# Cross-attention with adapter on one Trainium2 core: four of sixteen residual adds moved from VectorE to TensorE and ScalarE

## The chip, the cores and the metric

The kernel runs on one core of one Trainium2 chip. The metric is device microseconds of one execution; the median of three runs of the kernel before is 247.23 us (247.22 to 247.85). TensorE is called PE in the rows (PEld its weight loads), VectorE DVE, ScalarE ACT, GpSimd POOL, SyncE SP.

## What is computed

Two inputs x and ctx, 32 batches of 256 tokens by 256 features. The first layer is a cross-attention whose result for batch 0 alone (`att[0]`) is added to every batch. The second layer, cut to what matters here:

```python
norm_X, norm_F = layernorm(ctx), layernorm(x)          # F is the queries
attended = softmax(norm_F @ norm_X.T / 16) @ norm_X
h = gelu(attended @ fc1.T + fc1_b)                     # 4 values per token
cross = h @ fc2.T + fc2_b
n = layernorm(cross)
self_attended = softmax(n @ n.T / 16) @ n
return norm_F + gamma2 * (cross + gamma1 * self_attended)
```

The last line's sum with `norm_F`, the queries, is the place of the change.

## The kernel before, in words

Batches are worked on in sixteen pairs, and features lie on the partitions in the end: `Fall` holds the normalized queries of all 32 batches in SBUF, 128 partitions by 2 chunks of 256 tokens per batch, fp32. A first part (to about 175 us) normalizes, does the first attention, and saves per token four hidden values.

The second part, from about 175 us, handles the self-attention. Since `cross` has rank five, its products are small: operands cut into bf16 pieces, 36 to 60 rows high. Each engine runs its own loop over steps p = 0 to 20, and within a step everything is in the order of the code. The order on TensorE in step p: `maxima_turn(p)` (L1074), `scores(p+1)` (L1063), `turn(p+2)` (L1048), `shift(p)` (L1082), `keep_busy` (L873, small fp32 products into bank 5 that nobody reads), then in even steps `attend` (L1095) and `output_turn` (L1114), in odd steps `back` (L1104), and last `output(p-5)` (L1130). `output(n)` is four bf16 products per pair, with both members in two PSUM banks, 6 and 7 for nearly all n, so the next pair has to wait until the banks are read. Pair 13 goes to banks 2 and 3, pair 15 to banks 0 and 1.

VectorE in step p: `maxima(p+1)` (L564, a reduction over 1024 columns that needs `scores(p+1)`), then `collected` (L571, even) or `returned` (L576, L579, L581, odd), then `finish(p-5)` (L586): it adds the pair's 1024 PSUM columns to `Fall`, in place, 128x1024 fp32. After that in early steps some algebra for the second half of the batches, which `turn(8)` in step 6 waits for.

ACT in step p: `maxima_turned(p)` (L830), `turned(p+2)` (L800, the copy sT), `weights(p)` (L838, the exponential of 1024 columns), and in even steps `output_turned` (L845, the copy cT). ACT's copy of L786 belongs to the first part. POOL cuts the coefficients for `output_turn` in `output_cuts` (L700 to L707), after `returned` on VectorE. SP stores each batch of `Fall` (L293) in order, once `finish` of its pair is done.

An order written by hand is all there is: no planner. Waits are semaphores; TensorE's `maxima_turn` also waits for VectorE's copy OB (L576) in even steps, `output(n)` for `finish(n-1)`, `finish(n)` for `output(n)`.

Steps of the trace that the argument uses: TensorE's turn of the maxima for step 9 starts at 209.74, that for step 10 at 212.41, that for step 11 at 215.87.

Of the kernel before, what the change touches and what calls it, by code (L numbers as in the profile page):

```python
# [24 lines left out]
ALU = mybir.AluOpType  # L25
ACT = mybir.ActivationFunctionType
# [4 lines left out]
N = 256  # L31
D = 256
NT = N // P
DC = D // P
# [12 lines left out]
GROUP = TILES // 2  # L47
LATE = {20: (0,), 22: (1,), 23: (2,), 24: (3,), 25: (4,), 26: (5,), 27: (6,), 28: (7,), 29: (8,)}
NEXT = {0: (0,), 2: (1, 2), 3: (3, 4), 4: (5, 6), 5: (7, 8)}
ASIDE = ()  # L50
SBANK1 = (0, 1, 5)
SLOTS_L = ((0, 1, 3), (3, 1, 2), (5, 1, 1))
SLOTS_R = ((0, 3, 2), (1, 3, 2), (2, 1, 1))
# [18 lines left out]
def build(nc, x, ctx, x0t, c0t, wqt, wkt, wvt, params, out):  # L72
# [5 lines left out]
    def sem(name):  # L78
        return stack.enter_context(nc.semaphore(name))
# [111 lines left out]
    exp2_ok, o2_mm, o2_saved = sem("exp2_ok"), sem("o2_mm"), sem("o2_saved")  # L191
    o2T_ok, back_mm = sem("o2T_ok"), sem("back_mm")
    ct_mm, cT_ok, f_mm, fin_ok = sem("ct_mm"), sem("cT_ok"), sem("f_mm"), sem("fin_ok")
    aside_ok, added_ok = sem("aside_ok"), sem("added_ok")
    h_ok, co_ok, sC_ok, pads_ok = sem("h_ok"), sem("co_ok"), sem("sC_ok"), sem("pads_ok")
    out_done = sem("out_done")

# [41 lines left out]
        return bank[2 * (1 - p % 2) + m]  # L239

    def own_adds(n):
        return sum(i not in ASIDE for i in range(n))

    STORED = tuple(range(PAIRS))

    def result(n):
        return {13: (2, 3), 15: (0, 1)}.get(n, (6, 7))

    def results(n):
        a, _ = result(n)  # L250
        return psum[:, 512 * a:512 * (a + 2)]

    def aside(n):
        return XT[:, (n // 2) % 2, :, :].rearrange("p c n -> p (c n)")

    def pair(n):
        return Fall[:, 2 * n:2 * n + 2, :, :].rearrange("p b c n -> p (b c n)")
# [16 lines left out]
    @block.sync  # L274
    def _(sp):
        sp.dma_start(par[:, :], params).then_inc(par_in, 16)
        for dst, src, arrived in ((x0T, x0t, q_in), (wqT, wqt, q_in), (c0T, c0t, k_in), (wkT, wkt, k_in),
                                  (wvT, wvt, v_in)):
            sp.dma_start(dst[:, :, :], src).then_inc(arrived, 16)

        for p in range(PAIRS):
            if p >= SLOTS // 2:
                sp.wait_ge(t_mm, turns_to(p - SLOTS // 2, 1))
            for src, dst, arrived in ((c_d, cN, c_in), (x_d, xN, x_in)):
                for b in (2 * p, 2 * p + 1):
                    sp.dma_start(dst[:, b % SLOTS, :], src[b, :, :]).then_inc(arrived[b % SLOTS], 16)

        for n, b in ((n, b) for n in STORED for b in (2 * n, 2 * n + 1)):
            if n in ASIDE:
                sp.wait_ge(added_ok, ASIDE.index(n) + 1)  # L290
            else:
                sp.wait_ge(fin_ok, own_adds(n) + 1)
            sp.dma_start(out_d[b, :, :], Fall[:, b, :, :].rearrange("p c n -> p (c n)")).then_inc(out_done, 16)  # L293
        sp.wait_ge(out_done, 16 * B)

    @block.vector
    def _(dve):
# [292 lines left out]
        for p in range(2 * QUADS + 5):  # L590
            if p + 1 < PAIRS:
                maxima(p + 1)
            if p % 2 == 0 and 2 <= p < 2 * QUADS + 2:
                collected((p - 2) // 2)
            if p % 2 == 1 and 3 <= p < 2 * QUADS + 3:
                returned((p - 3) // 2)
            if p >= 5 and p - 5 not in ASIDE:
                finish(p - 5)
            for part in NEXT.get(p, ()):
                algebra(1, part)  # L600

    @block.gpsimd
    def _(pool):
# [102 lines left out]
            pool.wait_ge(sC_ok, 5 * q + 4)  # L706
            pool.tensor_tensor(to[:, :, 2 * CO:3 * CO], left, to[:, :, CO:2 * CO], ALU.subtract).then_inc(sC_ok, 1)  # L707

        def add_aside(n):
            pool.wait_ge(aside_ok, ASIDE.index(n) + 1)  # L710
            pool.tensor_tensor(pair(n), aside(n), pair(n), ALU.add).then_inc(added_ok, 1)

        right(0)
        for p in range(2 * QUADS + 5):
            if p == 4:
                right(1)
            if p % 2 == 1 and 3 <= p < 2 * QUADS + 3:
                output_cuts((p - 3) // 2)
            if p - 5 in ASIDE:
                add_aside(p - 5)  # L720

    @block.scalar
    def _(act):
# [102 lines left out]
        def maxima_turned(p):  # L826
            act.wait_ge(m_mm, p + 1)
            if p >= 2:
                act.wait_ge(s2m_mm, p - 1)
            act.activation(nm2T[:, p % 2, :], bank[5][0:2 * VW, 0:P // 2].bitcast(BF16), ACT.Copy).then_inc(m_ok, 1)  # L830
# [13 lines left out]
                act.wait_ge(f_mm, 2 * q - 2)  # L844
            act.activation(cT[:, q % 2, :], bank[4][:, 0:NT * P].bitcast(BF16), ACT.Copy).then_inc(cT_ok, 1)  # L845

        def set_aside(n):
            act.wait_ge(f_mm, n + 1)
            if ASIDE.index(n) >= 2:
                act.wait_ge(added_ok, ASIDE.index(n) - 1)  # L850
            act.activation(aside(n), results(n), ACT.Copy).then_inc(aside_ok, 1)

        for p in range(2 * QUADS + 4):
            if p < PAIRS:
                maxima_turned(p)
            if p == 0:
                applied(QUADS - 1)
            if p + 2 < PAIRS:
                turned(p + 2)
            if p < PAIRS:  # L860
                weights(p)
            if p - 5 in ASIDE:
                set_aside(p - 5)
            if p == 1:
                hidden(1)
            if p % 2 == 0 and p >= 4:
                output_turned((p - 4) // 2)

    @block.tensor
    def _(pe):  # L870
        def keep_busy(n, b):
            for _ in range(n):
                pe.matmul(bank[b][:, 0:P], ident[:, :], ident[:, :], start=True, stop=True)  # L873
# [241 lines left out]
            last.then_inc(ct_mm, 1)  # L1115

        def output(n):
            pe.wait_ge(cT_ok, n // 2 + 1)
            if n == 14:
                pe.wait_ge(fin_ok, own_adds(13))  # L1120
            elif n in (13, 15):
                pe.wait_ge(exp2_ok, PAIRS)
            elif n - 1 in ASIDE:
                pe.wait_ge(aside_ok, ASIDE.index(n - 1) + 1)
            elif n >= 1:
                pe.wait_ge(fin_ok, own_adds(n))
            for c in range(DC):
                for m in range(2):
                    rows = slice(SLOT * m, SLOT * m + SC)
                    last = pe.matmul(bank[result(n)[m]][:, c * N:(c + 1) * N], RT[rows, c * P:(c + 1) * P],  # L1130
                                     cT[rows, (n // 2) % 2, (n % 2) * N:(n % 2 + 1) * N], start=True, stop=True)
            last.then_inc(f_mm, 1)

        for b in range(B + 1):
# [31 lines left out]
        for p in range(2 * QUADS + 5):  # L1166
            if p < PAIRS:
                maxima_turn(p)
            if p == 0:
                keep_busy(3, 6)  # L1170
                apply(QUADS - 1)
            if p + 1 < PAIRS:
                scores(p + 1)
            if p == 0:
                apply_back(QUADS - 1)
            if p + 2 < PAIRS:
                turn(p + 2)
            if p < PAIRS:
                shift(p)
                keep_busy(5 if p < 5 else 2, 5)  # L1180
            if p % 2 == 0:
                if 2 <= p < 2 * QUADS + 2:
                    attend((p - 2) // 2)
                if 4 <= p < 2 * QUADS + 4:
                    output_turn((p - 4) // 2)
            elif 3 <= p < 2 * QUADS + 3:
                back((p - 3) // 2)
            if p >= 5:
                output(p - 5)
# [49 lines left out]
```

## Time and profile before

| | before |
|---|---|
| median of 3 runs | 247.23 us |
| profiled execution, its own time | 246.86 us |
| its span, first to last instruction | 245.1 us |
| mean granted TensorE clock | 0.957 |
| busy: PE, PEld | 214.2 us (87%), 154.2 us (63%) |
| busy: DVE, ACT, POOL | 198.0 us (81%), 148.9 us (61%), 124.4 us (51%) |
| L586, the adds, 16 | 19.4 us, mean 1221 ns |
| L564, reductions, 16 | 19.5 us, mean 1218 ns |

The busy shares are means over both parts. The page's slices, 40 of 6.1 us each, show tenths of busy time; the second part is slices 29 to 40:

```
PE   6989989677999999999999899999978569999750
DVE  6888858899999978789899999733558958998764
PEclk9999999999999999999999999999999759999955
```

The engines' rows have one digit per slice; PEclk is the granted clock in tenths. A timeline's row gives the start, the duration, the instructions merged into it, and in brackets the engine's idle time before it and what ended that. The ends of matmuls are modelled, so on TensorE the distance between starts is the safer number.

### The profile page before, as it was taken

What the parts mean: (1) busy time and instruction counts of PE and PEld (TensorE: products, weight loads), DVE (VectorE), ACT (ScalarE), POOL (GpSimd) and SP (SyncE); (2) the same over time, 40 slices, a digit from 0 to 9 for tenths busy, and PEclk for the clock granted to TensorE, in tenths of its full rate; (3) what the DMA queues carried; (4) which work ended last, traced back from release to release, by engine and by line L of the source; (5) the groups of instructions that cost most, each with busy time, mean ns of one, the idle gap of its engine ahead of it and who ended that gap; (6) DMA issues with size and microseconds to landing.
All of it is one profiled execution on the core that took longest, in us unless ns stands there. A gap on an engine that the chain in (4) does not pass through costs nothing.

```text
span 245.1 us, 4980 instructions
## 1 busy us (share of the span) xinstructions
PE 214.2 (87%) x1758; PEld 154.2 (63%) x1758; DVE 198.0 (81%) x391; ACT 148.9 (61%) x284; POOL 124.4 (51%) x184
## 2 busy tenths in 40 slices
PE   6989989677999999999999899999978569999750
PEld 6766548446878779697787787867645225554320
DVE  6888858899999978789899999733558958998764
ACT  2167856226778678596787968846775326666310
POOL 6000096776999999969698939200002522222220
PEclk9999999999999999999999999999999759999955
DMA  6990000242455514455243000000000022444566
GB/s 186 366 350 3 1 4 0 93 143 109 173 171 148 161 56 155 174 168 174 82 151 113 3 1 3 0 1 3 0 3 1 0 88 86 173 175 174 190 238 257
DMA packets 14712, 26.81 MB, mean 109 GB/s; under 512 B 1760, under 2 KB 1760, under 8 KB 14688
## 3 DMA queue, kind: packets, MB, share of 16 engines
q1 hardware_dynamic: 14688, 26.50, 31.2%
q8 instruction: 14, 0.23, 0.4%
q14 instruction: 10, 0.08, 0.1%
HBM read 18.11 MB, written 8.39 MB: 108 GB/s over the span
## 4 chain that ended last, share of the span: by engine, by line
PE 55%; DVE 28%; issue 8%; ACT 4%; POOL 2%; DVEq 0%; POOLq 0%; ACTq 0%
PE psum L981 15%; PE psum L918 7%; DVE bn L381 6%; DVE xN L401 6%; PE psum L989 5%; PE psum L873 5%; DVE nm L564 3%; PE psum L1019 3%; PE psum L1095 3%; PE psum L931 2%; DVE nmax L524 2%; PE psum L1001 2%; PE psum L946 2%; PE psum L959 2%; PE psum L888 2%
## 5 line engine op out<-in xcount | busy, mean ns | idle before, releaser
L981 PE MATMUL psum<-XT,Fall 128*128 128x256 f32 x256 | 60.9, 381 | 1.8 <-ACT Fall L763 1.8
L981 PEld LDWEIGHTS psum<-XT,Fall 128*128 128x128 f32 x256 | 46.1, 190 | 7.2 <-ACT Fall L763 2.2
L656 POOL TENSOR_SCALAR cN<-cN,nmean,rstd 128x256 f32<-128x256 f32 x64 | 38.5, 614 | 2.4 <-POOL rstd L643 2.3
L636 POOL TENSOR_TENSOR xN<-xN,tgt 128x512 f32<-128x512 f32 x28 | 35.7, 1278 | 1.6 <-DVE xN L401 1.6
L401 DVE TENSOR_SCALAR xN<-xN,bn,rstd 128x256 f32<-128x256 f32 x64 | 33.8, 571 | 0.7 <-POOL rstd L643 0.7
L786 ACT ACTIVATE PT<-psum 128x512 f32<-128x512 f32 x32 | 19.2, 599 | 24.3 <-PE psum L989 24.2
L700 POOL CAST sC<-co 128x160 bf16<-128x160 f32 x8 | 2.6, 322 | 61.6 <-DVE co L581 61.6
L793 ACT ACTIVATE E<-psum,nmax 128x256 f32<-128x256 f32 x64 | 26.8, 475 | 10.9 <-DVE nmax L524 10.9
L524 DVE TENSOR_REDUCE nmax<-psum 128x2 f32<-128x512 f32 x32 | 22.0, 686 | 13.7 <-PE psum L981 13.2
L643 POOL TENSOR_TENSOR rstd<-vps,minus_half 128x8 f32<-128x8 f32 (+1 forms) x16 | 25.0, 1564 | 15.4 <-DVE vps L392 15.3
L760 ACT ACTIVATE XT<-psum,b1s,w1s 128x512 f32<-128x512 f32 x32 | 23.1, 794 | 3.8 <-PE psum L918 3.8
L763 ACT ACTIVATE Fall<-psum,par 128x512 f32<-128x512 f32 x32 | 23.4, 797 | 3.2 <-PE psum L918 3.2
L873 PE MATMUL psum<-ident 128*128 128x128 f32 x144 | 23.3, 308 | 1.9 <-POOL ident L608 1.9
L873 PEld LDWEIGHTS psum<-ident 128*128 128x128 f32 x144 | 19.4, 208 | 5.5 <-issue 3.6
L586 DVE TENSOR_TENSOR Fall<-psum,Fall 128x1024 f32<-128x1024 f32 x16 | 19.4, 1221 | 4.2 <-PE psum L1130 4.2
L381 DVE BATCH_NORM_STATS2 bn<-cN 128x6 f32<-128x512 f32 x32 | 22.3, 695 | 0.4 <-DVE r L457 0.2
L381 DVE BATCH_NORM_STATS2 bn<-xN 128x6 f32<-128x512 f32 x32 | 21.9, 689 | 0.0
L564 DVE TENSOR_REDUCE nm<-psum 128x4 bf16<-128x1024 f32 x16 | 19.5, 1218 | 1.5 <-PE psum L1063 1.4
L989 PE MATMUL psum<-ident,E 128*128 128x128 f32 x128 | 20.2, 280 | 0.3 <-ACT E L793 0.2
L989 PEld LDWEIGHTS psum<-ident,E 128*128 128x128 f32 x128 | 14.3, 141 | 8.3 <-issue 6.3
L918 PE MATMUL psum<-ident,xN 128*128 128x128 f32 x128 | 17.1, 274 | 2.6 <-DVE xN L401 2.3
L918 PE MATMUL psum<-ident,cN 128*128 128x128 f32 x128 | 16.9, 274 | 0.1
(157 smaller groups left out, 348.5 us busy)
## 6 DMA issues: line engine op xcount, KB each, us to landing
cN<-ctx SPq DMA_DIRECT2D x32, 256.0 KB, 2.9
xN<-x SPq DMA_DIRECT2D x32, 256.0 KB, 4.2
out<-Fall SPq DMA_DIRECT2D x32, 256.0 KB, 2.3
x0T<-x0t SPq DMA_DIRECT2D x1, 256.0 KB, 2.6
wqT<-wqt SPq DMA_DIRECT2D x1, 256.0 KB, 2.9
c0T<-c0t SPq DMA_DIRECT2D x1, 256.0 KB, 3.7
wkT<-wkt SPq DMA_DIRECT2D x1, 256.0 KB, 4.8
wvT<-wvt SPq DMA_DIRECT2D x1, 256.0 KB, 5.0
```

The source lines that it names most:

```text
L381: dve.bn_stats(bn[:, (b // 2) % 4, side, b % 2, :], src[:, b % SLOTS, :].rearrange("p (t d) -> p d t", t=NT)).then_inc(st_ok, 1)
L401: dve.tensor_scalar(own, own, stat(p, 1, m, t, 1), root_of(p, 1, m, t), ALU.subtract, ALU.mult)\
L524: dve.tensor_reduce(nmax[:, b % 2, :], tiles(bank[SBANK1[b % 3]]), AX.X, ALU.max, negate=True)\
L564: dve.tensor_reduce(nm2[:, p % 2, :, 0:NT], scored(p).rearrange("p (m t k) -> p m t k", m=2, t=NT), AX.X, ALU.max, negate=True).then_inc(m ...
L636: pool.tensor_tensor(xN[:, b % SLOTS, :], xN[:, b % SLOTS, :], tgt2[:, :, :].rearrange("p t d -> p (t d)"), ALU.add).then_inc(y_ok, 1)
L643: pool.tensor_tensor(rstd[:, p % 4, sides, :].rearrange("p s k -> p (s k)"), vps[:, p % 4, sides, :].rearrange("p s k -> p (s k)"), minus_ ...
L656: pool.tensor_scalar(own, own, nmean[:, p % 4, NT * m + t:NT * m + t + 1], root_of(p, 0, m, t), ALU.add, ALU.mult)\
L793: act.activation(E[:, b % 2, t * N:(t + 1) * N], bank[SBANK1[b % 3]][:, t * N:(t + 1) * N], ACT.Exp, bias=nmax[:, b % 2, t:t + 1]).then_in ...
L873: pe.matmul(bank[b][:, 0:P], ident[:, :], ident[:, :], start=True, stop=True)
L918: last = pe.transpose(bank[TBANK[n % 3]][:, m * N + t * P:m * N + (t + 1) * P], z[:, (2 * p + m) % SLOTS, t * D + c * P:t * D + (c + 1) * ...
L981: last = pe.matmul(bank[SBANK1[b % 3]][:, t * N:(t + 1) * N], Fall[:, b, c, t * P:(t + 1) * P], XT[:, p % 4, c, m * N:(m + 1) * N], start= ...
L989: last = pe.transpose(bank[SBANK1[b % 3]][:, k * N + t * P:k * N + (t + 1) * P], E[:, b % 2, t * N + k * P:t * N + (k + 1) * P], ident[:, :])
```

## The change

For the pairs 1, 4, 7 and 10 the sum with the queries is made in PSUM: TensorE multiplies the four 128x256 pieces of `Fall` of the pair by the fp32 identity, before the output products accumulate onto them. ACT copies the two banks back into `Fall`, one member each, one step later: the first ahead of the copy sT, the second behind the exponential. VectorE does no add for these pairs, the next pair's `output` waits for the second copy, and SP stores each member after its own copy. In the steps of these four outputs `keep_busy` is left out. The wait for cT stands behind the identity products. An unused path (`ASIDE`, empty before) is removed with its helpers.

```diff
-ASIDE = ()
+SUMMED = (1, 4, 7, 10)
...
         for n, b in ((n, b) for n in STORED for b in (2 * n, 2 * n + 1)):
-            if n in ASIDE:
-                sp.wait_ge(added_ok, ASIDE.index(n) + 1)
+            if n in SUMMED:
+                sp.wait_ge(moved_ok, 2 * SUMMED.index(n) + b % 2 + 1)
             else:
                 sp.wait_ge(fin_ok, own_adds(n) + 1)
...
-            if p >= 5 and p - 5 not in ASIDE:
+            if p >= 5 and p - 5 not in SUMMED:
                 finish(p - 5)
...
-        def set_aside(n):
+        def moved(n, m):
             act.wait_ge(f_mm, n + 1)
-            if ASIDE.index(n) >= 2:
-                act.wait_ge(added_ok, ASIDE.index(n) - 1)
-            act.activation(aside(n), results(n), ACT.Copy).then_inc(aside_ok, 1)
+            act.activation(Fall[:, 2 * n + m, :, :].rearrange("p c n -> p (c n)"), bank[result(n)[m]], ACT.Copy)\
+                .then_inc(moved_ok, 1)
 
         for p in range(2 * QUADS + 4):
             if p < PAIRS:
                 maxima_turned(p)
+            if p - 6 in SUMMED:
+                moved(p - 6, 0)
             if p == 0:
                 applied(QUADS - 1)
             if p + 2 < PAIRS:
                 turned(p + 2)
             if p < PAIRS:
                 weights(p)
-            if p - 5 in ASIDE:
-                set_aside(p - 5)
+            if p - 6 in SUMMED:
+                moved(p - 6, 1)
...
         def output(n):
-            pe.wait_ge(cT_ok, n // 2 + 1)
             if n == 14:
                 pe.wait_ge(fin_ok, own_adds(13))
             elif n in (13, 15):
                 pe.wait_ge(exp2_ok, PAIRS)
-            elif n - 1 in ASIDE:
-                pe.wait_ge(aside_ok, ASIDE.index(n - 1) + 1)
+            elif n - 1 in SUMMED:
+                pe.wait_ge(moved_ok, 2 * SUMMED.index(n - 1) + 2)
             elif n >= 1:
                 pe.wait_ge(fin_ok, own_adds(n))
+            if n in SUMMED:
+                for c in range(DC):
+                    for m in range(2):
+                        pe.matmul(bank[result(n)[m]][:, c * N:(c + 1) * N], ident[:, :], Fall[:, 2 * n + m, c, :],
+                                  start=c == 0, stop=False, skip_group_check=True)
+            pe.wait_ge(cT_ok, n // 2 + 1)
             for c in range(DC):
                 for m in range(2):
                     rows = slice(SLOT * m, SLOT * m + SC)
                     last = pe.matmul(bank[result(n)[m]][:, c * N:(c + 1) * N], RT[rows, c * P:(c + 1) * P],
-                                     cT[rows, (n // 2) % 2, (n % 2) * N:(n % 2 + 1) * N], start=True, stop=True)
+                                     cT[rows, (n // 2) % 2, (n % 2) * N:(n % 2 + 1) * N], start=n not in SUMMED,
+                                     stop=True, skip_group_check=n in SUMMED)
             last.then_inc(f_mm, 1)
...
-                keep_busy(5 if p < 5 else 2, 5)
+                keep_busy(5 if p < 5 else 0 if p - 5 in SUMMED else 2, 5)
```

## Rows read from the trace of the kernel before

**Rows 1.** Windows: time and engines' busy us (instructions), PEclk, DMA share, GB/s.
```profile
210.00:216.00 6.00, 5.70 (x64) 3.00 (x60) 5.44 (x9) 3.96 (x8) 1.51 (x5) 1.00 0.47 171
216.00:222.00 6.00, 5.70 (x64) 3.04 (x63) 5.49 (x8) 3.89 (x8) 1.50 (x5) 1.00 0.46 170
```

**Rows 2.** Timeline of VectorE, 209 to 216 us: start, us, engine, line.
```profile
209.17 0.42 DVE L571 COPY wqT<-psum 128x256 f32<-128x256 f32 x1 [0.29 <-PE psum L1095]
209.80 1.22 DVE L586 TENSOR_TENSOR Fall<-psum,Fall 128x1024 f32<-128x1024 f32 x1 [0.20 <-PE psum L1130]
210.94 1.21 DVE L564 TENSOR_REDUCE nm<-psum 128x4 bf16<-128x1024 f32 x1
212.07 0.20 DVE L576 COPY OB<-psum 128x48 f32<-128x48 f32 x1
...
215.92 1.23 DVE L586 TENSOR_TENSOR Fall<-psum,Fall 128x1024 f32<-128x1024 f32 x1 [0.20 <-PE psum L1130]
```

**Rows 3.** Timeline of TensorE's matmuls, 209 to 216 us.
```profile
209.74 0.22 PE L1074 MATMUL psum<-identb,nm 128*64 128x128 bf16 x1
...
210.86 0.71 PE L873 MATMUL psum<-ident 128*128 128x128 f32 x4
211.41 0.38 PE L1104 MATMUL psum<-ident,wqT 128*128 128x128 f32 x2
211.72 0.39 PE L1130 MATMUL psum<-cT,RT 60*128 60x256 bf16 x4
212.41 0.22 PE L1074 MATMUL psum<-identb,nm 128*64 128x128 bf16 x1 [0.30 <-DVE OB L576]
...
213.54 0.71 PE L873 MATMUL psum<-ident 128*128 128x128 f32 x4
214.18 1.05 PE L1095 MATMUL psum<-PT,u 128*6 128x256 f32 x16
...
215.49 0.39 PE L1130 MATMUL psum<-cT,RT 60*128 60x256 bf16 x4
215.87 0.22 PE L1074 MATMUL psum<-identb,nm 128*64 128x128 bf16 x1
```

**Rows 4.** Timeline of TensorE's matmuls in the first part, 105 us.
```profile
105.04 1.89 PE L981 MATMUL psum<-XT,Fall 128*128 128x256 f32 x8
106.77 0.38 PE L1027 MATMUL psum<-ident,oTq 128*128 128x128 f32 x2
```

**Rows 5.** Timeline of ACT at 210 us, and the instructions of line 786.
```profile
209.99 0.27 ACT L830 ACTIVATE nm2T<-psum 64x128 bf16<-64x128 bf16 x1
210.64 0.60 ACT L800 ACTIVATE sT<-psum 128x512 bf16<-128x512 bf16 x1 [0.38 <-PE psum L1048]
211.14 1.02 ACT L838 ACTIVATE PT<-psum 128x1024 f32<-128x1024 f32 x1
...
L786 ACT ACTIVATE PT<-psum x32: 590/597/619, 55.7 to 169.9; 128x512 f32<-128x512 f32 x32
```

**Rows 6.** Timeline of TensorE from 199 us, and windows of the same stretch.
```profile
199.70 1.22 PE L873 MATMUL psum<-ident 128*128 128x128 f32 x4
200.85 1.89 PE L1095 MATMUL psum<-PT,u 128*6 128x256 f32 x16
...
203.22 0.41 PE L1130 MATMUL psum<-cT,RT 60*128 60x256 bf16 x4
...
199.00:203.00 4.00, 4.00 (x31) 1.81 (x28) 0.99 (x2) 1.57 (x2) 0.00 (x0) 0.50 0.08 26
203.00:204.00 1.00, 1.00 (x12) 0.37 (x10) 0.57 (x2) 0.68 (x2) 0.00 (x0) 0.85 0.00 0
```

**Rows 7.** Timeline of TensorE's matmuls in the tail.
```profile
229.72 0.39 PE L1130 MATMUL psum<-cT,RT 60*128 60x256 bf16 x4
...
232.36 0.40 PE L1114 MATMUL psum<-identb,sC 128*128 128x128 bf16 x4 [1.13 <-POOL sC L707]
```

**Rows 8.** Window of the tail, columns as in rows 1.
```profile
231.00:236.00 5.00, 1.93 (x21) 0.70 (x14) 3.58 (x7) 0.60 (x1) 1.93 (x8) 0.80 0.54 202
```

More of the change, by code:

```diff
@@ L193, in build @@
     ct_mm, cT_ok, f_mm, fin_ok = sem("ct_mm"), sem("cT_ok"), sem("f_mm"), sem("fin_ok")
-    aside_ok, added_ok = sem("aside_ok"), sem("added_ok")
+    moved_ok = sem("moved_ok")
     h_ok, co_ok, sC_ok, pads_ok = sem("h_ok"), sem("co_ok"), sem("sC_ok"), sem("pads_ok")
@@ L241, in own_adds @@
     def own_adds(n):
-        return sum(i not in ASIDE for i in range(n))
+        return sum(i not in SUMMED for i in range(n))
     STORED = tuple(range(PAIRS))
@@ L251, in results @@
         return psum[:, 512 * a:512 * (a + 2)]
-    def aside(n):
-        return XT[:, (n // 2) % 2, :, :].rearrange("p c n -> p (c n)")
     def pair(n):
@@ L707, in output_cuts @@
             pool.tensor_tensor(to[:, :, 2 * CO:3 * CO], left, to[:, :, CO:2 * CO], ALU.subtract).then_inc(sC_ok, 1)
-        def add_aside(n):
-            pool.wait_ge(aside_ok, ASIDE.index(n) + 1)
-            pool.tensor_tensor(pair(n), aside(n), pair(n), ALU.add).then_inc(added_ok, 1)
         right(0)
@@ L718, in _ @@
                 output_cuts((p - 3) // 2)
-            if p - 5 in ASIDE:
-                add_aside(p - 5)
     @block.scalar
@@ L861, in _ @@
                 weights(p)
-            if p - 5 in ASIDE:
-                set_aside(p - 5)
+            if p - 6 in SUMMED:
+                moved(p - 6, 1)
             if p == 1:
```

## The prediction

> **What bounds the kernel now.** I first read the page's slices: TensorE and VectorE are both nearly full between 204 and 228 us, where fourteen of the sixteen result pairs are still to come. All that the diff touches runs after 197 us, so the rest of the kernel is left alone. Then the windows of that stretch [rows 1]: in six microseconds TensorE is busy for 5.7, VectorE for 5.4 to 5.6, ACT for under 4. Two engines at over 90% can't both be waited for all the time, so the timelines must say which one has the slack.
>
> VectorE's timeline [rows 2] repeats every 6.13 us, which is two steps of the last loop. The add of pair 3 starts at 209.80, the next reduction at 210.94: 1.14 us is what one add takes from the queue, though the row says 1.22. VectorE waits 0.29 us for `attend` and 0.20 us for `output`, 0.5 us in a pair of steps. TensorE's timeline [rows 3] is one unbroken row of matmuls but for a single gap of 0.30 us ahead of 212.41, where the turn of the maxima waits for VectorE's copy OB; from the last product's start (211.72, four products at 0.33 us together) to that turn I count 0.33 us. So TensorE has 0.33 us of room in 6.13, and VectorE 0.5. Of TensorE's work 1.2 us in a pair of steps is filler (`keep_busy`, four instructions a step, 213.54 to 214.18 is 0.64 us; 210.86 to 211.41 is 0.55 us).
>
> **The change part by part.** In a summed pair n (1, 4, 7, 10) the step is p = n + 5.
>
> *VectorE loses four adds*, 1.14 us each. Were it alone the bound, the three in the steady part (the fourth lies ahead of a wait in the tail) would give 3.4 us.
>
> *TensorE gets four fp32 products with the identity per pair.* An fp32 matmul shows as two instructions in this trace: the eight of `score`, with the same form (128*128 by 128x256 f32), start at 105.04 and the next group at 106.77 [rows 4], so 1.73 us for eight, 216 ns each; their weight loads are hidden, and here too. It loses the filler of that step, 0.55 us in an odd step and 0.64 us in an even one. No row shows this product itself; the bounds are the filler's spacing of 160 ns at half the columns (8 x 0.16 = 1.28 us) and twice 216 ns at half clock (3.46 us). I take 1.73, from the row of the same form.
>
> *ACT gets two copies per pair*, 128x512 f32 out of PSUM. L786 is that form: 597 ns [rows 5]; back to back such an instruction takes some 0.51 us of the queue (sT at 210.64, exponential at 211.14). In step p = n + 6 the order on ACT becomes: maxima turned, first half, sT, exponential, second half. Counted from TensorE's turn of the maxima (209.74 in step 9), the maxima copy starts at +0.25, sT at +0.90, the exponential at +1.40 [rows 5]. The first half fits into the 0.38 us for which ACT waited before sT, and pushes it by about 0.06: sT +0.96, exponential +1.46, second half +2.40, its end +3.0.
>
> *The added wait.* `output(n+1)` on TensorE now waits for that second half instead of an add. In step 9 `output` starts at 211.72, +1.98 after the turn [rows 3]; that is the length of every odd step. So `output(2)` (step 7) and `output(8)` (step 13) would wait 3.05 - 1.98 = 1.07 us. Behind that wait stand all of the next step's TensorE work and, through it, VectorE's add and next reduction. In an even step `attend` and `output_turn` lie ahead of `output`: 212.41 to 215.49 is +3.08, so `output(5)` (step 10) doesn't wait. The exponential is 0.06 us late, and its readers (`scores` of p + 2, over 2 us on) don't see it.
>
> *The sum*, as shift of TensorE's queue against before:
> - Pair 1, step 6. The granted clock is 0.50 up to 203 and 0.85 over the microsecond after it, so it rises from 1.2 to 2.4 GHz at about 203.3, after 4 us of TensorE without a gap [rows 6]. The filler gone gives 1.15 us (199.70 to 200.85), so the identity products start at 203.22 - 1.15 = 202.07: three instructions at 432 ns reach the rise, five at 216 end at 204.45. 204.45 - 203.22 = +1.2 us.
> - Step 7, wait on ACT: 1.07, less the 0.33 us in which TensorE used to wait for OB: +0.74.
> - Pair 4, step 9: 1.73 - 0.55 - 0.33 = +0.85.
> - Pair 7, step 12: 1.73 - 0.64 = +1.09 (an even step ends in no gap).
> - Step 13, wait on ACT: +0.74.
> - Pair 10, step 15: 0. In the tail `output_turn` stood idle for 1.13 us for POOL's cuts before 232.36 [rows 7], whose chain starts from `back`, ahead of `output(10)` in the queue and 0.55 us earlier without filler. The products' 1.1 us go into that gap. ACT has nothing before its two halves in step 16: with `output(10)` some 1.2 us later than now (229.72, plus the products), they end about 1.1 us after it, under `attend` and `output_turn` (1.3 us). Both ends: 0 and +0.3.
>
> Together 1.2 + 0.74 + 0.85 + 1.09 + 0.74 = 4.6 us. VectorE's 3.4 us turn into idle time ahead of its reductions, because these need `scores`, which stand behind `output` on TensorE. The last three adds and the stores shift as they are; SP's separate waits for the halves release the summed pair's first store a little before its second, and stores queue there behind nothing else before the tail, so I cost them at nothing; were that cover gone it would be one store's landing, 2.3 us at most. The removed POOL helper never ran, the flag `skip_group_check` issues nothing, and the wait for cT moved behind the identity products was long met.
>
> The profiled execution took 246.86 us (span 245.1 and 1.76 around it), which gives 251.5; the median of the runs is 0.37 above it, and 247.23 + 4.6 = **251.8 us**.
>
> A rule that speaks for the change: in the steady window weight loads on TensorE are busy 3.0 us of 6 [rows 1]. The Trainium skill, Perfetto Trace Analysis, section Identifying the Most-Contended Engine, has it that matmul busy time is no measure of TensorE's headroom and weight-load busy share is. By that rule half of TensorE were free and VectorE the engine to unload, which is the first rival below. The sum above doesn't go by the busy share but by starts: within the 3.46 us from 212.41 to 215.87 no start waits for anything [rows 3].
>
> **The rivals.**
> - *VectorE is the bound* (other side). Place: VectorE's queue at steps 9 and 12, where the reduction would follow `collected` at once. It decides if the identity products cost TensorE less than filler and slack together, 0.55 + 0.33 = 0.88 us in an odd step, that is 110 ns an instruction. For it: 91% busy, and the chain passes VectorE in each step. Against: 216 ns in the nearest row. It gives 3 x 1.14 = 3.4 us: 243.8. Chance 0.07.
> - *It evens out*: products at 110 to 130 ns an instruction, below even the filler's 160, and no wait on ACT. Three groups then cost 0 to 0.16 us each, and VectorE can't run ahead of TensorE: about 247.5. Chance 0.04.
> - *Products only*: right on TensorE, but ACT's halves come in time (if `output`'s wait ends with the copy ahead of the exponential, or the exponential starts earlier). 4.6 - 1.5 = 3.1: 250.3. For it: ACT is under 70% busy. Against: the order on ACT. Chance 0.12.
> - *The clock*: pair 1's products run wholly at the lower level, since the filler ahead is gone: 3.46 in place of 2.38, +1.1: 252.9. For it: the level rose just as `output(1)` ran [rows 6]. Against: the same unbroken work runs, and the products are work too. A new 1.07 us gap could also lower it, but the tail's fall came where TensorE was busy for less than half of 231 to 236 [rows 8], and the gaps here stand amid full work. Chance 0.10.
>
> **How the numbers follow.** The forecast has 0.67. Some 0.3% (0.74 us) is what a measurement of this kernel can tell. All but the first two cases are slower: 0.89; the even case 0.04; faster 0.07. The range leaves out the fast and even cases (0.11) and little else: down to 249.3, products only with each of three groups 0.3 us cheaper, and up to 253.3, the clock case with 0.3 us from the tail and 0.1 from a hop.
>
> **What would show it.** Identity products eight per pair, 1.73 us at full clock; the period of steps 8 and 9 near 7 us; TensorE idle about 1.1 us in steps 7 and 13 for ACT; VectorE with some 1 us idle ahead of reductions at steps 9 and 12, released by TensorE; L586 twelve times. Wrong if the reductions follow VectorE's copies without a gap, if the halves end before `output` arrives, or if the last adds start before 240 us in the span.

## The result, and the profile after

The changed kernel takes **253.77 us** in the median of four runs (252.59 to 254.90) against 247.22 before: ratio 1.026 (95% interval 1.0199 to 1.0321), 6.55 us slower. The interval leaves no doubt that it is slower; whether by more than 2% these four runs don't settle. Forecast was 251.8, within 249.3 to 253.3, so the sign was right and the size too small. Run again later, the same kernel gave 255.68 (253.16 to 256.59), ratio 1.0322 (1.0258 to 1.0385). The kernel before scattered over 2.2 us in all its runs (246.13 to 248.30).

| | before | after |
|---|---|---|
| median | 247.22 us | 253.77 us |
| profiled execution, its own time | 246.86 us | 252.59 us |
| its span | 245.1 us | 250.8 us |
| the sixteen (twelve) adds, VectorE | 19.4 us | 14.5 us |
| instructions of the four pairs' identity products (line 1121) | none | 32 |

The page's slices of the changed kernel, 40 of 6.3 us each (the rows are TensorE, VectorE and the granted clock in tenths):

```profile
PE   6989979578999999999998999999886598998940
DVE  7888848999999888787999989443399827576364
PEclk9999999999999999999999999999998589998895
```

VectorE has become the engine with holes in the second part, and TensorE stays full. The clock has a dent (88) in slices 37 and 38, two slices ahead of the end, that the kernel before didn't have.

The instructions of the new lines, with min/median/max in ns, and the timeline of TensorE's matmuls (start, us, engine, line, merged count, and in brackets the idle time before them and what ended it). Line 1121 is the identity products, 1127 `output`, 1066 the turn of the maxima with which a step begins:

```profile
L1121 PE MATMUL psum<-Fall,ident x32: 379/379/741, 202.2 to 236.9; 128*128 128x256 f32 x32
...
L840 ACT ACTIVATE Fall<-psum x8: 577/595/603, 205.2 to 238.1; 128x512 f32<-128x512 f32 x8
```

```profile
202.18 2.27 PE L1121 MATMUL psum<-Fall,ident 128*128 128x256 f32 x8
204.39 0.39 PE L1127 MATMUL psum<-cT,RT 60*128 60x256 bf16 x4
204.71 0.24 PE L1066 MATMUL psum<-identb,nm 128*64 128x128 bf16 x1
...
207.70 0.39 PE L1127 MATMUL psum<-cT,RT 60*128 60x256 bf16 x4 [0.91 <-ACT Fall L840]
208.02 0.24 PE L1066 MATMUL psum<-identb,nm 128*64 128x128 bf16 x1
...
212.90 1.93 PE L1121 MATMUL psum<-Fall,ident 128*128 128x256 f32 x8
214.76 0.39 PE L1127 MATMUL psum<-cT,RT 60*128 60x256 bf16 x4
215.09 0.24 PE L1066 MATMUL psum<-identb,nm 128*64 128x128 bf16 x1
...
225.84 0.24 PE L1066 MATMUL psum<-identb,nm 128*64 128x128 bf16 x1
...
228.84 0.39 PE L1127 MATMUL psum<-cT,RT 60*128 60x256 bf16 x4 [0.91 <-ACT Fall L840]
229.16 0.24 PE L1066 MATMUL psum<-identb,nm 128*64 128x128 bf16 x1
...
233.89 0.24 PE L1066 MATMUL psum<-identb,nm 128*64 128x128 bf16 x1
```

These are the rows that answer to [rows 3] and [rows 6]. At full clock eight instructions take 1.86 us from their start to the next group's (212.90 to 214.76), 0.13 more than `score` in [rows 4]; in step 6, where the clock rose on the way, it was 2.21. In steps 7 and 13 TensorE stands idle for 0.91 us, and the releaser is ACT's copy, line 840. ACT in step 7, answering to [rows 5]:

```profile
204.99 0.27 ACT L821 ACTIVATE nm2T<-psum 64x128 bf16<-64x128 bf16 x1 [1.97 <-PE psum L1066]
205.16 0.58 ACT L840 ACTIVATE Fall<-psum 128x512 f32<-128x512 f32 x1
205.64 0.60 ACT L791 ACTIVATE sT<-psum 128x512 bf16<-128x512 bf16 x1
206.13 1.02 ACT L829 ACTIVATE PT<-psum 128x1024 f32<-128x1024 f32 x1
207.04 0.60 ACT L840 ACTIVATE Fall<-psum 128x512 f32<-128x512 f32 x1
```

The first half takes the gap ahead of sT, the exponential starts 1.42 us after the turn at 204.71, the second half at +2.33 and its row says that it ends at +2.93. `output` starts at +2.99. The forecast had +3.05.

What VectorE does with the time it was given (line 561 is the reduction):

```profile
205.32 1.23 DVE L561 TENSOR_REDUCE nm<-psum 128x4 bf16<-128x1024 f32 x1 [2.98 <-PE psum L1055]
...
215.70 1.22 DVE L561 TENSOR_REDUCE nm<-psum 128x4 bf16<-128x1024 f32 x1 [1.20 <-PE psum L1055]
...
226.46 1.22 DVE L561 TENSOR_REDUCE nm<-psum 128x4 bf16<-128x1024 f32 x1 [2.30 <-PE psum L1055]
...
243.70 3.49 DVE L583 TENSOR_TENSOR Fall<-psum,Fall 128x1024 f32<-128x1024 f32 x3 [1.48 <-PE psum L1127]
```

Three of the reductions wait 2.98, 1.20 and 2.30 us for TensorE's `scores`. So the time taken from VectorE has become idle time.

**Where the 5.7 us of span came from.** A step begins with the turn of the maxima on TensorE; the difference of the two profiles, less what it was one step before, is the price of the step:

| step begins | before | after | later by | new in the step before it | forecast |
|---|---|---|---|---|---|
| 6 | 195.51 | 195.77 | 0.26 | (nothing changed yet) | |
| 7 | 203.55 | 204.71 | 1.16 | +0.90, products of pair 1 | +1.2 |
| 8 | 206.28 | 208.02 | 1.74 | +0.58, wait for ACT | +0.74 |
| 9 | 209.74 | 211.50 | 1.76 | +0.02 | 0 |
| 10 | 212.41 | 215.09 | 2.68 | +0.92, products of pair 4 | +0.85 |
| 12 | 218.54 | 221.24 | 2.70 | +0.02, steps 10 and 11 | 0 |
| 13 | 222.06 | 225.84 | 3.78 | +1.08, products of pair 7 | +1.09 |
| 14 | 224.74 | 229.16 | 4.42 | +0.64, wait for ACT | +0.74 |
| 15 | 227.96 | 233.89 | 5.93 | **+1.51** | 0 |
| last three adds | 237.97 | 243.70 | 5.73 | -0.20 | 0 |

The five terms of the sum come to 0.90 + 0.58 + 0.92 + 1.08 + 0.64 = 4.12 us, forecast 4.62. Step 14 holds a term that the sum did not have. The windows of it (time, busy us and instructions of PE, PEld, DVE, ACT, POOL, granted clock, DMA share, GB/s):

```profile
226.00:230.00 4.00, 3.05 (x32) 1.59 (x31) 2.56 (x5) 2.93 (x6) 1.14 (x4) 1.00 0.26 99
230.00:233.00 3.00, 3.00 (x24) 1.32 (x20) 1.63 (x2) 1.02 (x1) 0.35 (x2) 0.52 0.45 163
233.00:234.00 1.00, 1.00 (x13) 0.56 (x9) 0.42 (x1) 0.33 (x1) 0.00 (x0) 0.72 0.48 180
```

TensorE's clock fell from 2.4 to 1.2 GHz at about 230.1, 1.3 us after the end of step 13's gap, though TensorE was working then, and it came back at 233.6. TensorE's work in between took nearly twice as long: `attend` in step 14 took 1.82 us from its start to the next group's, for 0.98 in the kernel before. The profiled run is the shortest of the four. The eight runs of this kernel, four here and four in e9, sort by their mean granted clock: 252.6 us at 0.959, 252.9 and 253.2 at 0.954, 254.6 and twice 254.9 at 0.945, 256.4 and 256.6 at 0.939.

### The profile page after: what moved, and what is told of

Its sections match the earlier page's. It is cut to its first block, busy times and chain, and to the rows that moved or that the text cites. A ratio compares the mean times of both kernels' runs of the same rounds, so it can differ in the third digit from the quotient of the medians.

```text
span 250.8 us, 5012 instructions
## 1 busy us (share of the span) xinstructions
PE 220.2 (88%) x1774; PEld 158.4 (63%) x1774; DVE 193.8 (77%) x387; ACT 152.7 (61%) x292; POOL 124.1 (49%) x184
## 4 chain that ended last, share of the span: by engine, by line
PE 54%; DVE 26%; ACT 8%; issue 6%; DMA 2%; POOL 1%; SPq 1%; DVEq 0%; POOLq 0%; ACTq 0%
PE psum L973 13%; PE psum L910 6%; DVE bn L378 6%; DVE xN L398 5%; PE psum L981 4%; PE psum L1087 3%; PE psum L1121 3%; PE psum L1011 2%; PE psum L865 2%; DVE nmax L521 2%; PE psum L923 2%; DMA wkT<-wkt 2%; DVE nm L561 2%; PE psum L993 2%; PE psum L938 2%
## 5 line engine op out<-in xcount | busy, mean ns | idle before, releaser
L865 PE MATMUL psum<-ident 128*128 128x128 f32 x128 | 20.8, 312 | 1.9 <-POOL ident L605 1.9
L865 PEld LDWEIGHTS psum<-ident 128*128 128x128 f32 x128 | 17.7, 214 | 4.6 <-issue 2.7
L583 DVE TENSOR_TENSOR Fall<-psum,Fall 128x1024 f32<-128x1024 f32 x12 | 14.5, 1220 | 3.8 <-PE psum L1127 3.8
```

## The experiments

All figures are medians; a ratio stands against runs of the kernel before on the same chip.

### The changed kernel's parts, one at a time (e1 to e4)

**e1**: the kernel before, without the filler of the four steps.

```diff
-                keep_busy(5 if p < 5 else 2, 5)
+                keep_busy(5 if p < 5 else 0 if p - 5 in (1, 4, 7, 10) else 2, 5)
```

> The kernel before, without the filler products of steps 6, 9, 12 and 15; nothing else changed. Theory A (TensorE's queue sets the pace there, and the changed kernel's own filler saving is worth what the prediction subtracted): step 6 gains up to 1.15 us, step 9 nothing (TensorE waits for the copy OB anyway), step 12 about 0.5, step 15 about 0.5, so 245.1 to 246.0. Rival C (the filler holds TensorE's clock up, and it is its absence that lowered the clock near 230 us in the changed kernel): the granted clock falls somewhere in 204 to 230 us, and the time is 248 or more.

Measured: 245.08 us (244.69 to 245.34) against 247.24, ratio 0.9917 (0.9888 to 0.9945). It is faster than both kernels, by the amount worked out from TensorE's queue: in the stretch, filler is on the path that sets the time. And in the profile the clock stayed up without it, from 203.9 to 234.6 us. Step 9 shows why the odd step gains nothing:

```profile
210.86 0.39 PE L1130 MATMUL psum<-cT,RT 60*128 60x256 bf16 x4
212.04 0.22 PE L1074 MATMUL psum<-identb,nm 128*64 128x128 bf16 x1 [0.79 <-DVE OB L576]
```

The wait for VectorE's copy OB has grown from 0.30 [rows 3] to 0.79 us; and step 9 lasts 2.67 us in both kernels; here VectorE's queue is the longer one. So VectorE sets the pace of such a step as soon as 0.5 us is taken from TensorE. The other direction, with work taken from VectorE, is what e2 was for.

**e2**: the changed kernel without identity products and without ACT's copies. It leaves the add out for four pairs and stores bare queries, and SP waits for `output` instead.

```diff
-                sp.wait_ge(moved_ok, 2 * SUMMED.index(n) + b % 2 + 1)
+                sp.wait_ge(f_mm, n + 1)
...
-            if p - 6 in SUMMED:
-                moved(p - 6, 0)
...
-            if p - 6 in SUMMED:
-                moved(p - 6, 1)
...
-            elif n - 1 in SUMMED:
-                pe.wait_ge(moved_ok, 2 * SUMMED.index(n - 1) + 2)
...
-            if n in SUMMED:
-                for c in range(DC):
...
-                                     cT[rows, (n // 2) % 2, (n % 2) * N:(n % 2 + 1) * N], start=n not in SUMMED,
+                                     cT[rows, (n // 2) % 2, (n % 2) * N:(n % 2 + 1) * N], start=True,
```

> The changed kernel without the identity products and without ACT's copies: the four summed pairs are stored as bare queries, their output products are made but not added. Theory A (TensorE is the bound): taking four adds (4.5 us) from VectorE gives at most the 0.3 to 0.5 us per pair of steps by which TensorE waits for VectorE, so 0 to 1.5 us less than e1. Rival D (VectorE is the bound): 3.4 us less than e1, near 242.

Measured: 251.26 us (251.11 to 251.50), ratio 1.0166 (1.0133 to 1.0199). Both expectations were wrong by far. Less work on VectorE made it 6.2 us slower than e1. The clock is enough to explain it; first e1's windows, then e2's:

```profile
199.00:203.00 4.00, 3.81 (x32) 1.39 (x32) 1.74 (x3) 1.85 (x3) 0.00 (x0) 0.50 0.20 75
204.00:212.00 8.00, 7.19 (x80) 3.71 (x78) 7.40 (x12) 5.60 (x9) 1.50 (x5) 1.00 0.41 154
```

```profile
199.00:203.00 4.00, 3.55 (x30) 1.38 (x32) 2.00 (x3) 1.59 (x3) 0.00 (x0) 0.50 0.27 101
204.00:212.00 8.00, 8.00 (x55) 3.93 (x51) 4.10 (x6) 3.44 (x6) 1.50 (x5) 0.50 0.35 131
216.00:222.00 6.00, 6.00 (x45) 2.56 (x41) 2.07 (x3) 2.52 (x5) 1.50 (x5) 0.50 0.34 125
```

In e1 the clock rose at about 203.9, in e2 at 212.3, and from 215.7 to 222.6 it was low once more. These are 15.3 us at half clock that e1 did not have, and 7.6 us of time if TensorE's work doubles in them (an estimate), against 6.1 us more of span. What VectorE's relief is worth at full clock can't be read from e2.

**e3**: the changed kernel without ACT's copies; the sums are left in PSUM and the queries are stored, with SP waiting for `output`.

```diff
-                sp.wait_ge(moved_ok, 2 * SUMMED.index(n) + b % 2 + 1)
+                sp.wait_ge(f_mm, n + 1)
...
-            if p - 6 in SUMMED:
-                moved(p - 6, 0)
...
-            if p - 6 in SUMMED:
-                moved(p - 6, 1)
...
-            elif n - 1 in SUMMED:
-                pe.wait_ge(moved_ok, 2 * SUMMED.index(n - 1) + 2)
```

> The changed kernel without ACT's copies: the identity products run, the sum stays in PSUM and the queries are stored. Theory A: it is slower than e2 by some 3 to 4 us (8 instructions of 216 ns in four places, less slack), 248.5 to 250.5, and without the two 0.9 us gaps in steps 7 and 13 the clock stays full to 234 us. If the products themselves cost the clock, it falls here too, and the time is 251 or more.

Measured: 249.48 us (249.10 to 249.89), ratio 1.0096 (1.0065 to 1.0128). As expected, by its range and by the clock, which in the profile stays at full from 203 to 240 us; only e2, from which the range was counted, came out slower and not faster. The products, with the filler and the adds of the four pairs gone, cost 2.2 us over the kernel before (4.4 over e1), and the rest of the change, 4.3 us at its first median, hangs on the copies: the two waits, and what the clock did behind them.

**e4**: the copies without the products; for four pairs bare output products overwrite the queries.

```diff
-            if n in SUMMED:
-                for c in range(DC):
-                    for m in range(2):
-                        pe.matmul(bank[result(n)[m]][:, c * N:(c + 1) * N], ident[:, :], Fall[:, 2 * n + m, c, :],
-                                  start=c == 0, stop=False, skip_group_check=True)
...
-                                     cT[rows, (n // 2) % 2, (n % 2) * N:(n % 2 + 1) * N], start=n not in SUMMED,
+                                     cT[rows, (n // 2) % 2, (n % 2) * N:(n % 2 + 1) * N], start=True,
```

> The changed kernel without the identity products: the four pairs' bare output products are copied over the queries by ACT. Theory A: the waits for the second half (0.9 us each, in steps 7 and 13) stay and cost 0.6 each after the slack: 0.5 to 1.5 us above e2. If these waits are what lowers the clock, it falls near steps 7 or 13 here too, and the time is 2 to 4 us above e2.

Measured: 249.06 and 249.82 us at a mean clock of 0.944 and 0.939, and three runs of 254.0 at 0.912 to 0.914. The first two lie 1.4 to 2.2 us below e2 (251.26 at 0.923 to 0.925), the others 2.7 above it, so it is inconclusive for the price of the waits, and shows once more that the time follows the clock. Only the long kind has a profile. In it the clock is low until 212.4 and from 215.8 to 222.6, as in e2. It falls a third time at 232.8, until 239.7, 2.4 us behind step 13's gap: TensorE waits 0.91 us for ACT ahead of 230.48. There are no identity products in this kernel, so they aren't needed for such a fall.

### What lowers the clock: the gaps or the missing filler (e5 to e7)

**e5**: six more filler instructions ahead of `back` in steps 7 and 13, to fill the gaps.

```diff
-                keep_busy(5 if p < 5 else 0 if p - 5 in SUMMED else 2, 5)
+                keep_busy(5 if p < 5 or p in (7, 13) else 0 if p - 5 in SUMMED else 2, 5)
```

> The changed kernel with six more filler instructions in steps 7 and 13, ahead of back, where TensorE stands idle 0.9 us for ACT's second half. They fit into that gap, so the order of everything else keeps its time. Theory G (the gaps are what lets the clock fall near 230 us): no fall there any more, the profiled span is 249 to 249.6 and the median 250.8 to 251.5, with less scatter than the changed kernel. Rival F (the fall comes from the filler left out of steps 12 and 15 and the gap has no part in it): the clock falls between 226 and 234 us as before and the median stays at 252.5 to 255.

Measured: 252.71 us (252.11 to 253.20), ratio 1.0232 (1.0204 to 1.0260). Of step 7's gap 0.24 us are left, and as much in step 13. Its row, and the windows from the first step after the clock's rise to the tail:

```profile
208.31 0.39 PE L1127 MATMUL psum<-cT,RT 60*128 60x256 bf16 x4 [0.24 <-ACT Fall L840]
...
203.00:205.00 2.00, 2.00 (x9) 1.37 (x7) 0.00 (x0) 0.00 (x0) 0.00 (x0) 0.69 0.00 0
205.00:241.00 36.00, 32.89 (x326) 18.44 (x325) 23.97 (x39) 21.54 (x38) 8.21 (x28) 1.00 0.41 153
```

The clock no longer falls in the steady part, all four runs have a mean clock of 0.956 or 0.957, and they lie within 1.1 us, where the changed kernel's eight runs spread over 4. From the turn of step 7 (205.32) to the turn of step 15 (233.03) it takes 27.7 us, against 29.2 in the changed kernel (204.71 to 233.89): the 1.5 us are back. The median came out 1.2 us above what I expected at most. In the profile 0.8 us of it is step 6, which took 9.74 us for 8.94: the clock rose later in this run, at 204.3 in place of 202.8, with the products of pair 1 at the lower level until then.

**e6**: both halves right behind the copy of the maxima.

```diff
             if p - 6 in SUMMED:
                 moved(p - 6, 0)
+                moved(p - 6, 1)
...
-            if p - 6 in SUMMED:
-                moved(p - 6, 1)
```

> The changed kernel with both of ACT's halves right behind the copy of the maxima, ahead of sT and the exponential. The second half then ends 1.5 us after the turn of the maxima, before output (at +2.0): the waits of steps 7 and 13 go. Theory G: about the time of e3 (249.5), 249.2 to 250.3, with the clock full to the tail. Rival H (the exponential, now 0.5 us later, holds up scores two steps on): the gap only moves, TensorE waits ahead of scores in steps 8 and 14, 251 or more.

Measured: 251.55 us (250.53 to 252.08), ratio 1.0181 (1.0149 to 1.0214). Both theories had a part:

```profile
206.34 0.24 PE L1065 MATMUL psum<-identb,nm 128*64 128x128 bf16 x1
...
208.35 0.39 PE L1126 MATMUL psum<-cT,RT 60*128 60x256 bf16 x4
208.81 0.22 PE L1065 MATMUL psum<-identb,nm 128*64 128x128 bf16 x1
209.39 0.40 PE L1054 MATMUL psum<-sT 36*128 36x256 bf16 x4 [0.36 <-ACT PT L829]
```

The wait of step 7 is gone (`output` 2.01 us after the turn), and 0.36 us of idle time has come up ahead of `scores` (line 1054) in step 8, for the exponential (line 829). The clock stays full from 205.5 to 243. It rose another 1.3 us later than in e5, which hides part of the gain.

**e7**: the changed kernel with the filler of before in every step.

```diff
-                keep_busy(5 if p < 5 else 0 if p - 5 in SUMMED else 2, 5)
+                keep_busy(5 if p < 5 else 2, 5)
```

> The changed kernel with the filler of before in all steps. It adds 0.55 to 0.64 us of queue at steps 9 and 12, 0.6 to 1.15 at step 6, nothing to 0.5 at step 15. Theory F (the missing filler lowered the clock): no fall near 230 us, which gives back 1.5 us, so about 253.5 with less scatter. Theory G (the gaps do it): the fall stays and the filler is on top, 254.5 to 256.

Measured: 255.42 us (253.21 to 256.45), ratio 1.0331 (1.0272 to 1.0389). That is Theory G's range, but the changed kernel itself lies anywhere from 252.6 to 256.6 us, so the time decides little; the profile does. The gap of step 7 and the fall behind it are there:

```profile
209.89 0.39 PE L1127 MATMUL psum<-cT,RT 60*128 60x256 bf16 x4 [0.91 <-ACT Fall L840]
```

```profile
209.00:212.00 3.00, 2.11 (x21) 1.19 (x21) 2.29 (x5) 1.96 (x5) 1.50 (x5) 1.00 0.40 150
212.00:216.00 4.00, 4.00 (x36) 1.58 (x37) 2.33 (x4) 1.53 (x4) 0.00 (x0) 0.57 0.35 131
```

Behind step 13's gap of 0.91 us the clock did not fall in this profile. The run of 253.21 us had a mean clock of 0.966 against the profiled run's 0.951, so it may have had no such fall at all; it has no trace. So filler elsewhere doesn't prevent the fall. It was absent where the gap was filled (e5) and where there was none (e3, e6), in one profile each, and the four runs of each of these kernels lie within 0.8 to 1.6 us. The gap lets the clock fall and doesn't make it fall every time.

### The scatter, the single pairs and a faster kernel (e8 to e12)

**e8**: the kernel before with no filler from step 5 on.

```diff
-                keep_busy(5 if p < 5 else 2, 5)
+                keep_busy(5 if p < 5 else 0, 5)
```

> The kernel before with no filler at all from step 5 on. If the clock stays up, VectorE's queue of 5.64 us a pair of steps sets the pace and each pair gains up to 0.5 us where e1 gained it in some only: 243.0 to 244.8. If the work left is too thin to hold the clock (as it was in e2), it stays low past 204 us or falls in between, and the time is 248 to 253.

Measured: two runs at 245.34 and 245.41, two at 250.5 and 250.6. In the profile of a run of the first kind the clock is low from 206.6 to 210.0 and from 223.6 to 227.1 us. The second expectation is met by two of the runs and, as for the clock, by the profile of one of the two short ones; the first is met by none. With less filler than e1 the clock is no longer held.

**e9**: the changed kernel once more, unchanged.

> The changed kernel once more, unchanged, beside the next three: the median 252.5 to 254.9. Where the run is above 254, theory G has a longer low stretch of the clock after step 7 or 13 than the 3.5 us of the first profile (230.1 to 233.3), or a later rise than 202.8; the rival, that the scatter has another source, has the same clock and other waits.

Measured: 255.68 us (253.16 to 256.59), ratio 1.0322 (1.0258 to 1.0385), 0.8 us above the expected range. The profiled run took 256.43:

```profile
207.74 0.39 PE L1127 MATMUL psum<-cT,RT 60*128 60x256 bf16 x4 [0.91 <-ACT Fall L840]
...
212.57 0.32 PE L1066 MATMUL psum<-identb,nm 128*64 128x128 bf16 x1
...
230.24 0.39 PE L1127 MATMUL psum<-cT,RT 60*128 60x256 bf16 x4 [0.91 <-ACT Fall L840]
...
235.94 0.32 PE L1066 MATMUL psum<-identb,nm 128*64 128x128 bf16 x1
...
237.63 3.46 PE L1121 MATMUL psum<-Fall,ident 128*128 128x256 f32 x8
241.03 0.39 PE L1127 MATMUL psum<-cT,RT 60*128 60x256 bf16 x4
```

```profile
209.00:213.00 4.00, 4.00 (x35) 1.68 (x33) 2.27 (x4) 2.18 (x4) 0.33 (x1) 0.64 0.41 153
230.00:234.00 4.00, 3.76 (x29) 1.85 (x33) 2.40 (x3) 1.48 (x3) 1.50 (x5) 0.57 0.38 139
234.00:241.00 7.00, 6.64 (x35) 3.58 (x24) 2.26 (x5) 1.89 (x3) 1.50 (x5) 0.51 0.30 111
```

The same two gaps of 0.91 us, ahead of 207.74 and 230.24, and now the clock falls after both: from 210.1 to 213.5, and from 230.6 to 240.8. The second time it takes pair 10's identity products with it, 3.40 us (237.63 to 241.03) in place of 1.93. Waits and instructions are those of the first profile; its 3.8 us more of span are the clock.

**e10**: pairs 4, 7 and 10 alone.

```diff
-SUMMED = (1, 4, 7, 10)
+SUMMED = (4, 7, 10)
```

> The changed kernel with pairs 4, 7 and 10 summed and pair 1 as before, its filler of step 6 included. Theory A, by the first profile after: the products of step 6 cost 0.9 us net and the wait of step 7 0.6, so 1.5 us less than the changed kernel, 251.5 to 253 as long as the clock still falls after step 13, and less scatter if the time of the clock's rise in the first group is a source of it. Rival: if pair 1's products while the clock is low cost more than that in the median, 3 us less or more, 250.5 or below.

Measured: 250.68 us (249.25 to 251.97), ratio 1.0116 (1.0055 to 1.0178): two runs at 249.3 with a clock of 0.965 or 0.966 and two at 252.0 with 0.952. The median lies below Theory A's range and 0.2 above the rival's. The profile of a run of the second kind has the fall after step 13's gap, from 229.5 to 232.9:

```profile
228.23 0.39 PE L1127 MATMUL psum<-cT,RT 60*128 60x256 bf16 x4 [0.91 <-ACT Fall L840]
```

The fall costs 1.51 us there (step 14 takes 4.73 us, for 3.22 in the kernel before), as in the changed kernel's first profile. It is not the whole 2.6 us between the two kinds: this run also had the lower clock from 48.6 to 52.0 us, in the first part, and its step 6 begins at 196.39, where the six profiles without such a stretch have 195.3 to 196.1. Leaving pair 1 out saved 3.1 us against the first median and 5.0 against e9, more than the 1.5 of its own two terms. It also takes away a gap after which the clock can fall, which is the likely reason and not a tested one.

**e11**: pair 10 alone.

```diff
-SUMMED = (1, 4, 7, 10)
+SUMMED = (10,)
```

> The changed kernel with pair 10 alone summed, all else as before. The prediction put this pair at 0 to 0.3 us, since TensorE waits 1.1 us for POOL behind it: 247.0 to 247.6. If the products can't hide there: 248 or more.

Measured: 247.21 us (246.64 to 247.84), ratio 1.0000 (0.9983 to 1.0018).

```profile
229.61 1.99 PE L1121 MATMUL psum<-Fall,ident 128*128 128x256 f32 x8
231.53 0.39 PE L1127 MATMUL psum<-cT,RT 60*128 60x256 bf16 x4
...
232.84 0.40 PE L1106 MATMUL psum<-identb,sC 128*128 128x128 bf16 x4
```

`output_turn` follows without a wait for POOL, at 232.84 where it was at 232.36 [rows 7], and 0.31 of these 0.48 us were there when step 15 began (228.27 against 227.96). So the 1.13 us of idle time have swallowed the products but for 0.17 us. The span is 245.1 as before, since in this run the tail was at full clock until 238.0, where the kernel before fell back at 234.0: the last adds start at 238.02 for 237.97.

**e12**: one filler product in place of two, beside e1's four steps with none.

```diff
-                keep_busy(5 if p < 5 else 2, 5)
+                keep_busy(5 if p < 5 else 0 if p - 5 in (1, 4, 7, 10) else 1, 5)
```

> The kernel before with no filler in steps 6, 9, 12 and 15 and one product (two instructions) in place of two in the other steps from 7 on. Between e1 (245.1) and e8 (245.4 or 250.5). If the clock holds: 244.0 to 245.0, VectorE then setting the pace. If it falls: 246 to 250.

Measured: 245.71 us, from 244.26 up, with one run at 252.49; the median lies between the two expectations. In its profile the clock is low from 224.3 to 227.7. The best run beats e1's best by 0.4 us; as a median it does not, and e1 is the version to keep: 2.2 us below the kernel before and 8.7 below the changed one.

The falls with thinner filler have gaps ahead of them too, and shorter ones: 0.55 and 0.60 us in e8, 0.33 us in e12, and 0.81 us ahead of e2's fall at 215.7. e1 kept full clock over a gap of 0.79 us, and the kernel before over gaps of 0.30 to 0.36. So the length of a gap alone doesn't decide it, and no run here isolates what does.

## Why the prediction was right or wrong

*What bounds it: right.* TensorE had 0.33 us of room per pair of steps, and what was put onto it beyond that room and the saved filler came out at the end nearly one for one. That its weight loads were busy for only half of the stretch was no sign of room. The rival with VectorE as the bound failed: three reductions stood waiting for TensorE for 1.2 to 3 us.

*The products: right, with some luck.* 0.92 and 1.08 us for pairs 4 and 7, forecast 0.85 and 1.09. The products took 1.86 us and not 1.73; in step 12 the groups around them stood closer by as much (0.24 us from `output_turn` to the products, where it was 0.34 to `output`), so the close match there is partly chance. Pair 1 took 0.90 for 1.2, since the clock rose at 202.8 in this run and not at 203.3. Pair 10 was free in sum; e11 shows 0.17 us of it ahead of `output_turn`, and a tail at a higher clock that gave them back.

*The added wait: right in place, a little long.* In steps 7 and 13 `output` starts 1.0 us later after the turn than it did, forecast 1.07; 0.91 us of that is idle. In step 10 there is no wait. Net 0.58 and 0.64 us, forecast 0.74.

*The clock: this step failed.* The sum had no term for it, and the clock was a rival at 0.10 that looked at the wrong place: pair 1's products. Of the new gaps the prediction said that a 1.07 us gap "could also lower it", and put it aside, because "the gaps here stand amid full work". In the runs that is what happened: in three profiles with the gaps (the changed kernel's two and e7's) the clock fell 0.3 to 2.4 us behind the end of at least one of them, and in e10's 1.2 us behind its only one. Filling most of the gaps (e5) or having none of this kind (e3, e6) left the clock at full until the tail in each profile. Its price was 1.5 us in the first profile and 3.8 more in the second. The tail of before, read as evidence of safety, was none: it only said that the clock falls when TensorE is mostly idle, not that it holds when it is mostly busy.

*The sum.* 4.6 forecast against 6.55 measured. In the profiles it is 4.1 us for the terms of the forecast, 0.26 from ahead of the change, 1.51 for the clock and -0.20 in the tail. The last 0.8 us is that the median run lies 1.2 us above its profiled one, and 0.4 in the kernel before; these longer runs have a lower mean clock, but no trace that shows where. The forecast's range ended at 253.3, 0.5 short of the median, because it took in the clock's rival once and for 1.1 us. Three numbers of the working are a little off and change nothing: by its own starts TensorE's room is 0.36 us and not 0.33, the range's lower end works out at 249.4, and the 2.3 us called a store's longest landing is the median (the longest is 4.4).

*The filler: right in size, missed as a hint.* That 1.2 us of each pair of steps on a full engine did nothing was in the prediction as a saving only. e1 shows that this saving alone is worth 2.2 us.

*What stays open.* e1 and e2 run the same TensorE instructions from 192 to 203 us within 0.3 us of each other, and the clock rises at 203.9 in one and 212.3 in the other. Nothing tried here says why. The profiles hold a pattern that no run tests: the clock had fallen to the lower level at 195.3 in e2 and at 193.7 in e1. In e4 it fell at 195.3 as well and rose at 212.4; these two are the kernels that fell so late and had neither filler nor identity products in step 6. e6, e7 and e10, which had one or both there, fell at 195.3 and were back at 205.5. The price of VectorE's relief at full clock was not measured.

## What to carry to other kernels

Where two engines are each over 90% busy, count starts on each within one period before moving work between them: the room on the one that takes the work, here 0.33 us of 6.13, is all that it takes for nothing, and what goes over it comes out at the end. When a change puts a new wait onto TensorE, price the wait twice: by its length, and by what a spell at 1.2 GHz costs behind it, and let the range hold both. And try taking filler out before moving real work; it may be on the path. Take it out by steps and run each several times: here four steps' filler was a gain in every run, and all of it (e8) a gain in two runs and a loss in two.

## What the hardware showed that I had not expected

An idle gap of 0.91 us on TensorE, amid steps in which no other gap was longer than 0.36 us, was followed by 3.4 us, once by 10.2 us, at the lower clock, and by nothing behind the same gap elsewhere (step 7 in the changed kernel's first profile, step 13 in e7's). Nor was the clock back because the engine worked: in e2 TensorE had no gap from 199.5 to 212.3 us and ran at 1.2 GHz all along. Taking four adds away from VectorE, with the lists of instructions of TensorE and ACT unchanged (e1 against e2), made the kernel 6.2 us slower.
